# Rope tables kept on chip, one copy of the keys, heads in turn, rope swaps begun by GpSimd

## What is computed

```python
B, S, E, H = (2, 256, 256, 16)      # shapes of the call: 1 x 2048 x 256
NOPE, ROPE, VD = (128, 64, 128)
LORA = 64
q = (x @ wq).reshape(b, s, H, QH).transpose(0, 2, 1, 3)
q_nope, q_pe = (q[..., :NOPE], q[..., NOPE:])
kva = x @ wkv_a
ckv, k_pe = (kva[..., :LORA], kva[..., LORA:])
ckv = ckv * rsqrt(mean(ckv * ckv) + EPS) * kv_norm_scale
kv = (ckv @ wkv_b)...
k_nope, v = (kv[..., :NOPE], kv[..., NOPE:])
q_pe = _rope(q_pe, cos, sin)
k_pe = _rope(k_pe[:, None, :, :], cos, sin)          # one for all heads
scores = einsum('bhqd,bhkd->bhqk', qs, ks_) * scale  # causal
out = einsum('bhqk,bhkd->bhqd', softmax(scores), v) ... @ wo

x = L0_attn_x
xn = _layernorm(x, axis=-1)
s = attention(xn)
g = silu(down(silu(gate(xn)) * up(xn)))
x = x + s * g
```

## Time and profile before

| | |
|---|---|
| median of 3 runs | 1118.76 us (1116.97 to 1122.3) |
| the profiled execution | 1120.68 us |
| its span, first to last instruction | 1118.9 us |
| TensorE busy | 985.6 us, 88% |
| VectorE busy | 831.2 us, 74% |
| ScalarE busy | 714.0 us, 64% |
| GpSimd busy | 662.8 us, 59% |
| granted TensorE clock, mean | 0.95 of full |
| SP's DMA queue, share of 16 engines | 89.6% |

### The profile page before, as it was taken

One profiled execution on the slowest core, in us unless ns is written; L12 is line 12 of the kernel. 1 busy time (PEld: TensorE's weight loads), 2 busy tenths in 40 slices (PEclk: granted clock), 3 DMA queues, 4 the chain that ended last, 5 costly groups with the idle time before them and its releaser, 6 DMA issues.

```text
span 1118.9 us, 26420 instructions
## 1 busy us (share of the span) xinstructions
PE 985.6 (88%) x10576; PEld 842.8 (75%) x10576; DVE 831.2 (74%) x1359; ACT 714.0 (64%) x1033; POOL 662.8 (59%) x448
## 2 busy tenths in 40 slices
PE   6864898989988988999889998998899986989998
PEld 5743787778777877788778877876688775878887
DVE  6674687988787877878798779887888885873134
ACT  1335567776676767677677677776677774863232
POOL 3736766766576675756685658565857684422331
PEclk7777899999999999899999999999999998999999
DMA  5118899999999999999999999999999899992001
GB/s 146 38 40 168 152 186 197 197 197 184 184 187 199 189 187 185 202 184 188 189 207 185 197 190 206 180 192 178 202 178 211 179 192 207 178 176 76 1 20 57
DMA packets 600042, 184.92 MB, mean 165 GB/s; under 512 B 574960, under 2 KB 586864, under 8 KB 599920
## 3 DMA queue, kind: packets, MB, share of 16 engines
q1 hardware_dynamic: 595440, 182.57, 89.6%
q10 hardware_dynamic: 4480, 0.66, 0.4%
...
## 4 chain that ended last, share of the span: by engine, by line
PE 34%; DMA 24%; DVE 17%; POOL 10%; SPq 6%; ACT 5%; issue 4%; ACTq 1%; POOLq 0%
DMA pT<-hl 19%; PE s_ps L637 12%; PE s_ps L535 9%; DVE hl L948 5%; PE slot_ps L535 5%; DVE part_max L939 5%; POOL hl L1099 5%; ACT hl L743 3%; DMA sinT<-sinT_dram 2%; SPq L464 2%; ACT prob L809 2%; PE o_ps L653 2%; SPq L477 2%; PE o_ps L535 2%; PE o_ps L654 2%
## 5 line engine op out<-in xcount | busy, mean ns | idle before, releaser
L1099 POOL TENSOR_TENSOR hl<-prob,hl 128x1024 f16<-128x1024 f32 x128 | 274.5, 2144 | 228.3 <-ACT hl L743 224.4
L743 ACT ACTIVATE hl<-prob 128x1024 f16<-128x1024 f32 (+7 forms) x384 | 295.9, 804 | 160.3 <-DMA pT<-hl 159.6
L809 ACT ACTIVATE prob<-s_ps,neg_max 128x1024 f32<-128x1024 f32 (+7 forms) x384 | 316.7, 859 | 101.4 <-DVE neg_max L942 46.6
L939 DVE TENSOR_REDUCE part_max<-s_ps 128x1 f32<-128x1024 f32 (+7 forms) x256 | 243.7, 985 | 93.4 <-PE s_ps L637 74.4
L948 DVE TENSOR_TENSOR hl<-prob,hl 128x1024 f16<-128x1024 f32 (+7 forms) x256 | 255.9, 1035 | 62.4 <-ACT hl L743 62.1
L653 PE MATMUL o_ps<-v,pT 128*128 128x65 f16 x2176 | 231.8, 194 | 51.0 <-DMA pT<-hl 39.3
L653 PEld LDWEIGHTS o_ps<-v,pT 128*128 128x128 f16 x2176 | 205.4, 97 | 58.0 <-DMA pT<-hl 45.9
L654 PE MATMUL o_ps<-v,pT 128*128 128x64 f16 x2176 | 232.2, 196 | 0.0
L655 PE MATMUL o_ps<-v,pT 128*128 128x65 f16 x2176 | 231.1, 193 | 0.0
L655 PEld LDWEIGHTS o_ps<-v,pT 128*128 128x128 f16 x2176 | 205.6, 100 | 0.0
L654 PEld LDWEIGHTS o_ps<-v,pT 128*128 128x128 f16 x2176 | 204.8, 98 | 0.0
...
## 6 DMA issues: line engine op xcount, KB each, us to landing
...
q_swap<-q_pe SPq DMA_DIRECT2D x128, 64.0 KB, 2.1
pT<-hl SPq DMA_TRANSPOSE x256, 5.2
...
```

The lines of the kernel that those rows point to most:

```text
L743: return nc.scalar.activation(dst, src, ACT.Copy)
L809: nc.scalar.activation(prob_of(u, m), score_bank(u, m), ACT.Exp, bias=neg_max[:, r:r + 1]).then_inc(exp_done, 1)
L939: nc.vector.tensor_reduce(part_max[:, u % 2, m:m + 1], src, AX.X, ALU.max).then_inc(part_done, 1)
L1099: return lambda: nc.gpsimd.tensor_tensor(dst, a, b, op)
```

## The change

- **Tables.** `cosT` and `sinT` become 128 x 2048 and are loaded once, at the start; `load_tables` leaves the loop.
- **Keys.** One `K_hi`, `K_lo` instead of one for each head: four key jobs in setup instead of eight. The queries' rows are laid alike for both heads (rope above, latent below).
- **Query jobs.** `qA3` and `qB3` (one head's rope and latent part in one product) replace `pe3` and `lat3`. TensorE's products are as many; ScalarE copies 64 rows four times for a group, where it copied 128 rows once and 64 rows twice.
- **Heads.** `head_of(u)` is `u % 2`; a step `k // 2` serves both heads.
- **Rope sum.** GpSimd's `.2` adds 64 rows (head A) in place; head B's 64 rows are added by VectorE (`rope_of_b`, into `pe_b`), a new wait of VectorE for `rope .1` and of GpSimd for `rope_b`.
- **Swaps.** The four transfers of a group are issued by GpSimd at the head of `rope .0`.
- **Order.** All four tables of jobs and steps are new; the output of a pair is taken in the pair itself but for `outT3` and `outP3`, so five `out` jobs instead of nine remain for the feed-forward stage. The feed-forward loads move from k = 5 to 6, the first use of them from k = 6 to 8.

```diff
-        cosT = ab("cosT", [P, BANK])
-        sinT = ab("sinT", [P, BANK])
+        cosT = ab("cosT", [P, S])
+        sinT = ab("sinT", [P, S])
+        pe_b = ab("pe_b", [LORA, 2, BANK])
...
             load(0)
             load_wo(0)
-            load_tables(3, 0)
-            swap(3, 0)
-            load_tables(0, 0)
-            swap(0, 0)
-            load_tables(2, 0)
+            for g in GROUP_ORDER:
+                load_tables(g)
             for u in range(NU):
                 pair, k = divmod(u, PU)
                 turn_first(u)
-                for name in jobs_at(u - 1):
-                    if name[0].startswith("pe"):
-                        swap(int(name[0][2:]), name[1])
-                if u in TABLES_AT:
-                    load_tables(*TABLES_AT[u])
                 turn_rest(u)
...
+            def swap(g, pair):
+
+                half = ROPE // 2
+                pool.wait_ge(hi_done, after("hi", (f"qB{g}", pair)))
+                n = group_no(g, pair)
+                if n >= 1:
+                    before = GROUP_ORDER[(n - 1) % NG], (n - 1) // NG
+                    pool.wait_ge(pool_done, POOL.after((f"rope{before[0]}.2", before[1])))
+                    pool.wait_ge(rope_b, n)
+                for i in range(4):
+                    a, b = slice(i * half, (i + 1) * half), slice((i ^ 1) * half, (i ^ 1) * half + half)
+                    pool.dma_start(q_swap[a, :], q_pe[b, :]).then_inc(swapped, 16)
...
+            def rope_of_b(g, pair):
+
+                n = group_no(g, pair)
+                dve.wait_ge(pool_done, POOL.after((f"rope{g}.1", pair)))
...
+                nc.vector.tensor_tensor(pe_b[:, n % 2, :], pe[ROPE:P, n % 2, :], q_swap[ROPE:P, :], ALU.add).then_inc(rope_b, 1)
...
-POOL_NEXT = {2: ["wpe_hi"], 3: ["wpe_lo"], 4: ["wkvs"], 7: rope(3)[:2], 8: [rope(3)[2], "A3hi"], 9: ["A3lo"], 10: rope(0)[:2],
+POOL_NEXT = {1: ["wkvs"], 6: ["wpe_hi"], 7: ["wpe_lo"], 10: rope(3)[:1], 11: rope(3)[1:] + ["A3hi"], 12: ["A3lo", rope(0)[0], "B3hi"],
+             13: ["B3lo"] + rope(0)[1:], 14: side("A", 0), 15: side("B", 0)}
```

More of the change, by code:

```diff
@@ L139, in jobs_at @@
             jobs += [(name, pair - 1) for name in JOBS_BEFORE.get(k, ())]
-        jobs += [(name, pair) for name in (JOBS_OWN_LAST if last else JOBS_OWN).get(k, ())]
+        jobs += [(name, pair) for name in JOBS_OWN.get(k, ()) if (name, pair) not in OUT_LAST]
         if last:
@@ L199, in steps_at @@
     last = pair == PAIRS - 1
-    own = POOL_FIRST if pair == 0 else POOL_OWN_LAST if last else POOL_OWN
-    steps = [(name, pair) for name in own.get(k, ())]
+    steps = [(name, pair) for name in POOL_OWN.get(k, ())]
     if last:
@@ L204, in steps_at @@
     else:
[L205 to L217 removed]
+        steps += [(name, pair + 1) for name in POOL_NEXT.get(k, ())]
+    return steps
 POOL = Steps(POOL_SETUP + [name for u in range(NU) for name in [("low", u)] + steps_at(u)])
```

268 lines of the change are left out of this document (124 added, 144 removed).

## The result

| | before | after |
|---|---|---|
| median of 4 runs each | 1117.87 us | 1128.26 us |
| lowest to highest | 1115.93 to 1122.3 | 1124.15 to 1136.06 |
| ratio to before, 95% interval | | 1.0096 [1.0051, 1.0141] |
| profiled execution (its span) | 1120.68 (1118.9) | 1124.75 (1122.9) |

The forecast was 1096 and faster; the kernel became slower. From the page of the profile after: busy time by engine (us, share of the span), two of the DMA queues (packets, MB, share), the HBM traffic and the chain that ended last.

A forecast was written before the change was run, and what follows sets the result against it. Transposes waiting on SP's DMA queue were taken to bound attention, with GpSimd's low half close behind. Terms -17.7 - 18.7 + 8 + 7 - 2.4 = -23.8 us from 1120.68 gave 1096.9, forecast as 1096, range 1045 to 1150.

The forecast's parts named there:

- The swaps' issue on GpSimd: d, GpSimd's time to begin one swap transfer: 0.9 us, between 0.65 and 1.25; sum moves 128 us per us.
- Rival C: Dear swap issue (d from 1.09) makes lists at k = 4, 12 last 12 us or more; kernel slower; chance 0.26.
- Tables and swaps off SP's queue: Units with table loads or swaps shrink to 6.05 us: 7.9 and 9.3 us a pair gone from SP's queue.
- GpSimd's lists: Steps after a low half: 7.5 us at k = 2, 10; 6.7 at 3, 5, 11, 13; 10.4 at 4, 12.
- The step that failed: Pairs 2 to 7: eight units last as GpSimd's lists, eight 6.05 us each; 112.0 us a pair against 114.95, -17.7 in all.
- no compute engine is full: Attention, pairs 2 to 7 before: VectorE 82% and GpSimd 66% busy, while the DMA share is over 1.
- VectorE: Attention pairs: rope_of_b adds 4 x 0.69 = 2.8 us to 94.7, giving 97.5 us busy a pair.
- First pair and last pair: First attention pair falls from 129.2 to 110.5 us, -18.7; last pair, 99.0 before, gains 7 us.
- Behind: Feed-forward stage after attention: four output jobs leave a stage that TensorE bounds, -2.4 us.
- Rival B: Attention pairs: GpSimd's lists don't bind at all, pairs reach the floor of 101.6 us, about 1020 us; chance 0.07.
- D: Units with tables or swaps are long from their jobs; the 2 us return as VectorE's wait, 1119 us; chance 0.08.
- The signs named: Expected in the new profile if right: unit lengths, 0.9 us swap issues, waits, DMA share below 1, first scores near 76.

The follow-up runs named there:

- a_tables_back: Changed kernel with the table loads put back on SP's queue between the transposes, behind each group's second rope step; 1128.1 us, ratio 1.0065.
- a_swap_sp: Changed kernel with the swaps begun by SP's queue again, between a unit's two transposes, tables staying on chip; 1132.7 us, ratio 1.010.
- a_steps_short: Changed kernel with GpSimd's rope and split steps on one column instead of 512 from the second pair on; 1065.7 us, ratio 0.950.
- a_early_load: Changed kernel with the load of a pair's query and key-value weights begun half a pair earlier, at k = 8 instead of k = 0; 1123.0 us, ratio 1.000.
- a_rope_b_short: Changed kernel with VectorE's rope_of_b adding one column instead of 512 from the second pair on; 1100.8 us, ratio 0.982.
- b_tables_once: Kernel before, with no tables loaded from the second pair on and all compute instructions kept; 1073.9 us, ratio 0.957.
- c_spread2: Changed kernel with GpSimd's steps spread over all units, weight loads and some query jobs earlier, the wkvT job in k = 3; 1094.8 us, ratio 0.975.

## Why the prediction was wrong

**The swaps' issue on GpSimd** (d = 0.9, "midway"): 0.507, below the lower bound of 0.65 that I took from SP's queue. By the prediction's own 128 us for each us of d this is 50 us in favour: the forecast would have been 1046, and the real error is 82, not 32. Rival C's price of an issue that lets VectorE pass first shows nowhere: 507 ns in the mean over 96, and 2.01 us for the four at 465.54, which VectorE's two low halves overlap. What the prediction cited for it of the Trainium skill, SBUF — State Buffer, section SBUF: two separate sides, is said there of VectorE's 2-port modes, a condition that the prediction left out; the instructions that overlap here are `tensor_tensor` with both inputs in SBUF. The other citation, the 1 us and 0.6 us of the Trainium skill, DMA: Bandwidth & Descriptors, Specifications, is of the time to the first byte. The prediction set SP's 0.65 and its own d beside it, but these are what a transfer costs the engine that begins it, and that section does not speak of it.

**Tables and swaps off SP's queue** (-7.9 and -9.3 a pair): right in size to 0.4 us for the kernel before, and right that the wait `ACT hl <- DMA pT` goes. Wrong as terms to be added: a_tables_back shows the tables' worth in the new kernel as 1.4 us a pair at most, and a_swap_sp the place of the swaps as nothing that the medians can tell.

**GpSimd's lists**: the formula at d = 0.507 gives 6.0 (k = 2, 10), 6.7 (3, 5, 11, 13), 8.9 (4, 12). Measured means are 6.9 and 7.4; 7.1, 7.1, 6.4, 7.1; 9.2 and 8.9. So its long lists came out as foreseen, in part by luck: k = 4 and 12 hold a wait of GpSimd for VectorE's `pe_b` that the formula does not have (16.3 us in 12 units, 1.14 at 465.54), and in return single steps were shorter there than their means of before (`QA_lo` 1.27 for 1.47, `QB_hi` 1.03 for 1.25).

**The step that failed** is "I take these eight units as GpSimd's own and the other eight as plain: 62.6 + 48.4 + 0.9". Means by unit, us:

| k | 0 | 1 | 2 | 3 | 4 | 5 | 6 | 7 | 8 | 9 | 10 | 11 | 12 | 13 | 14 | 15 |
|---|---|---|---|---|---|---|---|---|---|---|---|---|---|---|---|---|
| before | 7.0 | 6.8 | 8.1 | 5.7 | 6.0 | 5.8 | 8.1 | 6.2 | 7.7 | 8.4 | 5.9 | 8.0 | 8.8 | 6.0 | 8.3 | 8.3 |
| after | 7.3 | 7.1 | 6.9 | 7.1 | 9.2 | 7.1 | 6.6 | 7.1 | 6.1 | 5.9 | 7.4 | 6.4 | 8.9 | 7.1 | 7.7 | 6.7 |
| a_steps_short | 7.3 | 7.2 | 7.1 | 8.0 | 7.4 | 6.3 | 5.9 | 6.6 | 6.1 | 5.8 | 7.1 | 6.0 | 7.1 | 6.2 | 6.0 | 6.4 |

Only k = 8 and 9 are plain. Together the eight are 5.2 us a pair above their 48.4 + 0.9 = 49.3, all of it in k = 0, 1, 6, 7, 14 and 15. k = 2 and 10 are 2.4 above their lists; with 1.3 for the rest that is the 8.9 between 105.7 (the formula at the true d) and 114.56. What holds the long ones differs. The units k = 0, 4 and 14 of one pair after, columns as in the earlier trace rows:

```profile
434.50:442.02 7.52, 7.41 (x106) 6.49 (x105) 6.78 (x13) 6.25 (x9) 2.15 (x1) 1.00 0.97 150
...
463.08:472.21 9.13, 8.94 (x117) 7.74 (x116) 8.90 (x15) 5.70 (x9) 7.74 (x8) 1.00 1.04 181
...
534.06:541.64 7.58, 4.89 (x51) 3.60 (x48) 6.08 (x8) 5.07 (x7) 7.21 (x5) 1.00 0.78 147
```

In k = 0 and 1 GpSimd has next to nothing to do, and with its steps gone these two stay as long. What lengthens them is mainly the load of weights that stands between them on SP's queue: with it elsewhere (a_early_load) they take 6.4 and 6.2 us. Of the 2.3 us that they are above two plain units, 1.8 go with it; the prediction had 0.9 a pair for it. TensorE is busy throughout in either kernel, so its full row in k = 0 is no proof that it holds the unit: it runs 106 products here and 76 there, and catches up or runs ahead of the transposes. Still, "no compute engine is full" left TensorE out, though it had 629.90 of 689.67 in the earlier trace rows. Its 609 us in six pairs of the quickest versions are 6.3 a unit, more than the 6.05 that I took for eight of them.

In k = 4 VectorE is full (8.90 of 9.13). In k = 14 GpSimd is busy for 7.21 of 7.58 us, but it is not what ends the unit: its next low half is over at 540.09, 1.55 us earlier. VectorE's, ScalarE's and TensorE's rows in that unit:

```profile
532.41 2.17 DVE L866 TENSOR_TENSOR pe_b<-pe,q_swap 64x512 f32<-64x512 f32 x1
534.61 2.15 DVE L918 TENSOR_TENSOR hl<-prob,hl 128x128 f16<-128x128 f32 x2
537.93 1.11 ACT L769 ACTIVATE prob<-s_ps,neg_max 128x1024 f32<-128x1024 f32 x1 [1.48 <-DVE neg_max L907]
539.10 0.50 PE L601 MATMUL s_ps<-K_hi,QA_hi 128*128 128x512 f32 x1 [2.14 <-ACT prob L769]
```

`rope_of_b` and two low halves of 128 columns, 0.69 and 0.28 us each at their shortest, stand 4.3 us together beside GpSimd's steps. The maximum behind them comes late, so does ScalarE's exponential, and TensorE stands for it 2.14 us; its weighing of two units earlier, for which the next transpose waits, ends at 541.6 (this wait of SP's queue is 19.9 us, 13 times, in the six pairs). So here GpSimd holds the unit through VectorE. k = 4, 6 and 14 become shorter without GpSimd's steps.

**VectorE** ("4 x 0.69 = 2.8 us a pair on 94.7, 97.5"): 105.0. The missing 7.5 are 4 x (1.34 - 0.69) = 2.6 of `rope_of_b` itself, (231.9 - 202.6) / 6 = 4.9 of longer low halves (sums over their eight forms). I saw in the earlier trace rows that the same step costs 1.25 or 1.38 and took it for GpSimd's matter; that VectorE loses time in such a meeting too, and that more steps beside it cost VectorE, was not priced. a_rope_b_short shows 27 us by the medians, 2.1 a pair in the profiles, for what stood in the sum as covered.

**First pair and last pair**: +7.6 and +2.5 off, in line with units of 7.4 instead of 6.9 in the first and feed-forward loads two units later. **Behind**: four output jobs less gave nothing that can be seen; not looked into.

**The rivals.** Rival C had the right sign and the right wait (`ACT prob <- POOL hl`, 64.9 us) but the wrong price: its list was to be 12 us by a dear issue. Rival B's floor of 101.6 was never reached; TensorE's 609 us in six pairs are as much. D (nothing moves) is close to the time and wrong as a mechanism. That 1128 lies between 1045 and 1150 is luck: the top of that range stood for a dear issue, and the issue was cheap. **The signs named**: k = 0 and 1 at 6, no; k = 8 and 9, yes; k = 4 and 12 at 10 or more, no, 9.2 and 8.9; DMA share below 1, hardly, 1.00 for 1.07; first scores near 76, yes, 74.7 us. Neither of the two signs of being wrong came (k = 12 at 8 or less, plain units at 8), though the forecast was.

**What stays open.** a_swap_sp has the transfers of b_tables_once and takes 59 us more. 27 would be `rope_of_b`, if it costs there what it costs in the changed kernel; c_spread2 shows that much of the rest is the order of steps and jobs. How the loss divides between waiting inside VectorE's instructions and longer lists of GpSimd is not separated. Heads in turn and the one copy of the keys were not tried alone, and the kernel before could not hold all tables beside its two copies of the keys.
